# A two-layer graph network on one core: node order and loads ahead of the edge check, a re-dealt message sum in layer 0, and layer 1's pass as loops with four row buffers

## What is computed

```python
edge_index = jnp.stack([src, dst])
h = jnp.maximum(_layernorm(x, axis=-1), 0.0)
x = x + _L0_gnn_ref(h, ..., node_type_3, src, dst, edge_type_6, 4)
h = jnp.maximum(_layernorm(x, axis=-1), 0.0)
x = x + _L1_gnn_ref(h, edge_index, W, att_src, att_dst, bias, gamma, beta)
```

## Time and profile before

| what | value |
|---|---|
| median of 3 runs | 4574.36 us (4572.99 to 4576.31) |
| the profiled execution | 4572.91 us, its span 4571.2 us |
| busy share of the span | PE 57%, DVE 66%, ACT 34%, POOL 49% |
| mean granted TensorE clock | 0.789 |

### The profile page before, as it was taken

The page is one execution under the profiler, slowest core; times in us unless marked ns, Lnnn a source line. Parts: engine busy times, 40 slices in busy tenths (PEclk is TensorE's granted clock), DMA queues, the critical chain, the costliest instruction groups (busy, mean ns, idle before and its releaser), DMA issues. The chain is left out here.

```text
span 4571.2 us, 55327 instructions
## 1 busy us (share of the span) xinstructions
PE 2583.8 (57%) x10078; PEld 1666.5 (36%) x10079; DVE 3014.4 (66%) x6013; ACT 1552.4 (34%) x3956; POOL 2235.5 (49%) x2256
## 2 busy tenths in 40 slices
PE   0099956666666761000477776666355556656553
PEld 0055533433443430000255554343244444444432
DVE  3344445555555556999899997766466666666667
ACT  0234433333333332320133333333234343443443
POOL 1422257777777770000233333222477777777751
PEclk9999977777777675555699998998678777777776
DMA  6356699999999993000466664000466666666652
GB/s 205 107 229 257 260 305 312 313 312 314 312 312 314 312 312 91 0 0 0 137 198 193 200 195 130 17 16 16 94 183 193 187 192 186 192 195 187 192 156 91
DMA packets 584267, 847.44 MB, mean 185 GB/s; under 512 B 137427, under 2 KB 478815, under 8 KB 577301
## 3 DMA queue, kind: packets, MB, share of 16 engines
q0 software_dynamic: 128032, 450.69, 30.8%
q1 hardware_dynamic: 456110, 395.43, 27.7%
HBM read 549.59 MB, written 297.50 MB: 185 GB/s over the span
## 5 line engine op out<-in xcount | busy, mean ns | idle before, releaser
L1804 POOL DMA_INDIRECT g_rows<-x1t,srci x880 | 850.0, 966 | 286.7 <-issue 258.1
L903 POOL DMA_INDIRECT rows<-kv,kvi x880 | 838.6, 953 | 287.8 <-issue 246.9
L949 PE MATMUL psD<-qs,hot 128*128 x1760 | 703.6, 528 | 256.1 <-DVE prod L990 188.7
L990 DVE TENSOR_TENSOR prod<-rows,psD 128x256 f32<-128x256 f32 x880 | 365.6, 417 | 481.3 <-DMA rows<-kv,kvi 329.2
L1240 POOL TENSOR_TENSOR wv<-vrows,wgt 128x1024 f32<-128x1024 f32 x110 | 220.2, 2002 | 846.0 <-DMA vrows<-val_v 669.3
L1958 PE MATMUL g_psM<-g_rows,g_hot 128*128 128x264 f32 x1760 | 558.9, 471 | 78.7 <-DVE g_rows L2076 69.6
L949 PEld LDWEIGHTS psD<-qs,hot 128*128 128x128 f32 x1760 | 385.3, 253 | 522.5 <-issue 316.7
L1320 PE MATMUL psM<-wv,vhot 128*128 128x260 f32 x1760 | 445.3, 396 | 146.7 <-DVE run L1339 139.8
L1958 PEld LDWEIGHTS g_psM<-g_rows,g_hot 128*128 128x128 f32 x1760 | 383.8, 229 | 170.8 <-issue 96.3
L969 ACT ACTIVATE off<-psB,npiota 128x256 f32<-128x256 f32 x440 | 207.8, 472 | 688.6 <-PE psB L940 686.3
L1320 PEld LDWEIGHTS psM<-wv,vhot 128*128 128x128 f32 x1760 | 317.8, 190 | 274.1 <-DVE run L1339 227.5
(11 more groups left out here) (395 smaller groups left out, 4324.5 us busy)
## 6 DMA issues: line engine op xcount, KB each, us to landing
val_v<-rows SPq DMA_DIRECT2D x220, 512.0 KB, 5.2
vrows<-val_v SPq DMA_DIRECT2D x220, 512.0 KB
sums_v<-g_run SPq DMA_DIRECT2D x110, 528.0 KB
g_drow<-drow_v SPq DMA_DIRECT2D x55, 512.0 KB
rows<-kv,kvi POOLq DMA_INDIRECT x880, 5.1
g_rows<-x1t,srci POOLq DMA_INDIRECT x880
g_ndt<-nodeb SPq DMA_DIRECT2D x440, 6.0 KB
hsort<-blank SPq DMA_DIRECT2D x4, 1690.0 KB, 14.4
```

Source lines behind the costliest of these rows:

```text
L903: nc.gpsimd.indirect_dma_start(out=rows[:, k], out_offset=None, in_=table, in_offset=bass.IndirectOffsetOnAxis(ap=index[:, i * SLOTS + k:i ...
L949: nc.tensor.matmul(psD[:, k % 4, 0:cols], hot[:, t % 2, j * P:(j + 1) * P], node[:, ds(blk[t], 1)].rearrange("p o d -> p (o d)"), start=Tr ...
L990: ins = nc.vector.tensor_tensor(prod[:, k % 4], rows[:, k, 0:D], psD[:, k % 4, 0:D], ALU.mult)
L1804: nc.gpsimd.indirect_dma_start(out=rows[:, i % NBUF, k, 0:ROW1], out_offset=None, in_=dr["x1t"], in_offset=bass.IndirectOffsetOnAxis(ap=v[ ...
```

## The change

Four parts:

1. **Order and loads of the prologue.** The node types and `x` are now loaded by ACT's queue in `consts`; the blank fill of `hsort` by four DMAs is gone, and 5 indirect DMAs write only the rows that no node fills. The places of the nodes are worked out in `order_edges`, ahead of the sortedness test. In `prepare_edges` DVE starts with the node statistics; POOL scatters 24 blocks of nodes, then fetches the 4 record tiles, then scatters the other 25; SP loads the projection's weights there instead of at the head of `project`.
2. **Layer 0's sum.** The last of the four `vhot` groups moves from DVE to ACT (four Abs into `vfar`, one Relu). DVE's adds now stand in two runs of four, not four runs of two, and POOL's `weigh` waits until the `vhot` groups of that half turn are done on DVE.
3. **Layer 1's pass.** `walk` writes the first and the last chunks out and puts 48 chunks in a hardware loop of 12 turns with four chunks each (SP, ACT, PE and DVE loop over the steps 2 to 49, POOL over the chunks 4 to 51). There are four row buffers and four index buffers `ids`, filled by one more DMA a chunk; semaphores are split so that most waits of a chunk compare with `i`, `i + 1` or `q + 1`.
4. **Tables in one place.** Several SBUF tables share their room (`early`, `ex = sq`, `raw` in `stage`); `rank_edges` works in 20 pieces instead of 16, but does not run on these inputs.

The core of the diff:

```diff
 SB = 51
+PADS = 5
 HROW = D + 4
 HB = 6
+EARLY = 24
 EPS = 1e-5
 SLOPE = 0.2
...
+            done(nc.gpsimd.memset(c["ti"][:], T))
+            done(nc.gpsimd.memset(xs[:, NB - 1], 0.0))
...
-        @block.sync
-        def _(sp):
-            sp.wait_ge(sem, 2)
-            for f in range(4):
-                sp.dma_start(dr["hsort"].rearrange("(s f p) d -> f p s d", p=P, f=4)[f],
-                             c["blank"][:, f].unsqueeze(1).to_broadcast([P, (SB + 1) // 4, HROW])).then_inc(c["blank_in"], 16)
+        @block.scalar
+        def _(act):
+            act.wait_ge(sem, 1)
+            act.dma_start(c["ti"][0:NB - 1, :], ntype[0:(NB - 1) * P].rearrange("(b p) -> b p", p=P)).then_inc(c["t_in"], 16)
+            act.dma_start(c["ti"][NB - 1:NB, 0:NLAST], ntype[(NB - 1) * P:N].rearrange("(b p) -> b p", b=1)).then_inc(c["t_in"], 16)
+            act.wait_ge(sem, 2)
+            act.dma_start(xs[:, 0:NB - 1], x[0:(NB - 1) * P].rearrange("(b p) d -> p b d", p=P)).then_inc(c["x_in"], 16)
+            act.dma_start(xs[0:NLAST, NB - 1], x[(NB - 1) * P:N]).then_inc(c["x_in"], 16)
...
+                    tt, tsc, stt, copy = (nc.vector.tensor_tensor, nc.vector.tensor_scalar, nc.vector.scalar_tensor_tensor, nc.vector.tensor_copy)
+                    tm = o["tm"]
+                    dve.wait_ge(c["t_in"], 32)
+                    step(copy(tf[:], c["ti"][:]))
+                    for t in range(T):
+                        step(tsc(tm[:, t], tf[:], float(t), None, ALU.is_equal))
+                        step(nc.vector.tensor_tensor_scan(count[:, t], c["ones"][0:NB], tm[:, t], 0.0, ALU.mult, ALU.add))
...
+                for k in range(PADS):
+                    nc.gpsimd.indirect_dma_start(out=dr["hsort"], out_offset=bass.IndirectOffsetOnAxis(ap=o["padi"][:, k:k + 1], axis=0),
+                                                 in_=c["blank"][:, k], in_offset=None).then_inc(s_pad, 16)
+
+                def records():
...
+                    if b == EARLY:
+                        records()
...
+                load_weights(sp, weights, given)
...
                 tt, tsc = nc.vector.tensor_tensor, nc.vector.tensor_scalar
-                dve.wait_ge(s_init, 12)
-                dve.wait_ge(s_dma, 19 * 16)
+                dve.wait_ge(c["x_in"], 32)
+                for b in range(NB):
+                    nc.vector.bn_stats(stats[:, b], xs[:, b]).then_inc(s_bn, 1)
+                dve.wait_ge(s_bn, NB)
+                for b in range(NB):
+                    nc.vector.bn_aggr(mv[:, b], stats[:, b]).then_inc(s_ag, 1)
+                dve.wait_ge(s_init, 10)
...
+                    g = NG - 1
+                    for k in range(GS):
+                        ins = nc.scalar.activation(far[:, k], c["iota"][:], ACT.Abs, scale=-1.0, bias=v["dr"][:, ds(i * SLOTS + (g * GS + k), 1)])
+                    ins.then_inc(far_done, 1)
+                    act.wait_ge(far_done, i + 1)
+                    act.wait_ge(m_done, i * V8 + 2 * g + 2)
+                    nc.scalar.activation(hot[:, g * GS:(g + 1) * GS], far[:], ACT.Relu, bias=1.0, scale=-1.0).then_inc(last_hot, 1)
+
                 def turn(i, first=False):
 
                     for g in range(NG):
+                        if g == 2:
+                            places(i)
                         beside(i, g)
                         if g >= 2:
...
+                        pool.wait_ge(hot_done, i * (NG - 1) + min(g + 1, NG - 1))
...
-                            pe.wait_ge(hot_done, i * NG + t // 2 + 1)
+                            if t // 2 < NG - 1:
+                                pe.wait_ge(hot_done, i * (NG - 1) + t // 2 + 1)
+                            else:
+                                pe.wait_ge(last_hot, i + 1)
...
-                                                ALU.is_equal).then_inc(hot_done, 1)
-
-                        if g >= 2:
-                            add(i, 2 * g - 4)
-                            add(i, 2 * g - 3)
+                    for g in range(0, NG, 2):
+                        weigh(dve, nc.vector, i, g)
+                        places(i, g)
+                        if g + 1 < NG - 1:
+                            places(i, g + 1)
+                        if g:
+                            for t in range(4):
+                                add(i, t)
                         elif not first:
-                            add(i - 1, 2 * g + 4)
-                            add(i - 1, 2 * g + 5)
+                            for t in range(4, V8):
+                                add(i - 1, t)
                 turn(0, True)
...
 NCH = NC // CH
-NBUF = 3
...
+
+    def place(n):
+        return n, n % NBUF, n // NBUF
+    for n in range(first, lo):
+        step(lambda d: place(n + d))
+    with engine.Fori(0, (hi - lo) // NBUF) as t:
+        for k in range(NBUF):
+            step(lambda d: (t * NBUF + (lo + k + d), (lo + k + d) % NBUF, t + (lo + k + d) // NBUF))
+    for n in range(hi, last):
+        step(lambda d: place(n + d))
+
+
...
+                    i, m, q = at(0)
+                    pool.wait_ge(ids_in[m], 16 * (q + 1))
                     for g in range(NGRP):
-                        if i >= NBUF:
-                            pool.wait_ge(sum_done, CV * (i - NBUF) + 2 * g + 2)
+                        if from_(i, NBUF):
+                            pool.wait_ge(sum_done[2 * g + 1], i - (NBUF - 1))
+                        pool.sem_inc(opened, 1)
                         for k in range(g * GRP, (g + 1) * GRP):
                             nc.gpsimd.indirect_dma_start(
-                                out=rows[:, i % NBUF, k, 0:ROW1], out_offset=None, in_=dr["x1t"],
-                                in_offset=bass.IndirectOffsetOnAxis(ap=v["srci"][:, i * CH + k:i * CH + k + 1], axis=0)).then_inc(got[i % NBUF], 16)
+                                out=rows[:, m, k, 0:ROW1], out_offset=None, in_=dr["x1t"],
+                                in_offset=bass.IndirectOffsetOnAxis(ap=ids[:, m, k:k + 1], axis=0)).then_inc(got[m], 16)
+                walk(pool, gather, 0, 4, 52, NCH)
 
...
+                def places(i, m, q):
+                    if from_(i, NBUF):
+                        sp.wait_ge(got[m], 16 * CH * q)
+                    sp.dma_start(ids[:, m], v["srci"][:, ds(i * CH, CH)]).then_inc(ids_in[m], 16)
...
+                def add(i, m, q, t):
+                    dve.wait_ge(sum_done[t], i + 1)
+                    if t:
+                        dve.wait_ge(run_done[t - 1], i + 1)
+                    if t % 4 == 0 and from_(i, 1):
+                        dve.wait_ge(saved[t // 4], i * 16)
                     before = run[:, t - 1] if t else base[:]
...
-                places_of_nodes(0)
-                for i in range(-2, NCH):
-                    if chunk(i):
...
+        ex = sq
         psS = tmp.enter_context(nc.psum_tensor("psS", [P, 3, 512], F32))
```

More of the change, by code:

```diff
@@ new lines, in _ @@
+                    step(nc.vector.tensor_reduce(blocks[:], over[:], AX.X, ALU.add))
+                    step(copy(end[:, 0:1], blocks[:, 0:1]))
+                    step(tt(end[:, 1:2], blocks[:, 0:1], blocks[:, 1:2], ALU.add))
+                    step(stt(out=offset[:, 1:T], in0=end[0:NB], scalar=float(P), in1=offset[:, 1:T], op0=ALU.mult, op1=ALU.add))
+                    for t in range(T):
+                        step(stt(out=count[:, t], in0=count[:, t], scalar=offset[:, t:t + 1], in1=tm[:, t], op0=ALU.add, op1=ALU.mult))
@@ L861, with edge_scores @@
 NI = NC // SLOTS
[L864 removed]
+def edge_scores(nc, c, dr, v, layer, table, index, node, width, node_in, early):
     L = layer
@@ L1732, with chunk, from_, walk @@
 SPL = 3
+def chunk(i):
+    return not isinstance(i, int) or 0 <= i < NCH
+def from_(i, n):
+    return not isinstance(i, int) or i >= n
+def walk(engine, step, first, lo, hi, last):
+    def place(n):
[7 more added lines that the diff above has]
+        step(lambda d: place(n + d))
 def attend_layer1(nc, c, dr, v):
@@ L1851, in _ @@
                     if chunk(i):
                         save(i, 1)
+                for n in range(3):
+                    places(n, n, 0)
+                sp.wait_ge(init, 5)
+                nodes(0, 0, 0)
+                nodes(1, 1, 0)
+                row_flags(0, 0, 0)
+                walk(sp, step, -2, 2, 50, NCH)
                 for u in range(2):
@@ L2139 @@
+                places_of_nodes(0, 0, 0)
+                walk(dve, step, -2, 2, 50, NCH)
+                tail = (NCH - 1, (NCH - 1) % NBUF, (NCH - 1) // NBUF)
+                add(*tail, 6)
+                add(*tail, 7)
 G7 = 7
```

718 lines of the change are left out of this document (368 added, 350 removed).

## The result

| | us |
|---|---|
| before, median of 4 runs | 4575.34 (4572.99 to 4582.33) |
| after, median of 4 runs | 4459.6 (4455.82 to 4473.02) |
| ratio | 0.975, 95% interval 0.9726 to 0.9773 |
| the profiled executions | 4572.91 and 4455.82, spans 4571.2 and 4453.9 |

The change made the kernel faster by 2.5%, 116 us, where 138 were forecast: 4459.6 lies inside the stated range (4408 to 4482) and 4.6 outside the main case's own (4415 to 4455). The later runs fell on other chips, and on one of those the very same kernel is slower than before, by 1.1%. That is the main finding of this study and stands under the experiments; first comes the trace of this chip, by the prediction's own steps.

What follows compares the result with a forecast made beforehand. DVE was taken to bound layer 0's sum, POOL's gather stream layer 1's pass, a chain the prologue. Prologue -48, sum -92, layer 1 +2 gave -138: 4436 us for the median, range 4408 to 4482.

Steps and rivals of the forecast that it cites:

- main case: Whole kernel: prologue, sum and layer 1 terms hold, 4436 us for the median, own range 4415 to 4455, chance 0.62.
- E: Rival in layer 1's pass: DVE's semaphore waits, as register operations, make DVE pass POOL's pace; +235, 4671 us, chance 0.04.
- wrong outright: Sign in layer 1's pass: POOL's gathers come to wait for anything but their own stream; no size given.
- Start of `prepare_edges`: Prologue: block starts at 41.9, 2 us earlier, bounds +5 and -11.8; by the skill's rule 0.
- First scatter: Prologue, `prepare_edges`: the first scatter to `hsort` comes 25 us after the block's start, at 66.9.
- Scatters and fetches: Prologue: 49 scatters 68.8 us, four record fetches among them 5.1, slowing beside DVE 3.5; last scatter ends at 144.3.
- rival D: Prologue gives 20 us less, by an edge path late at the fetches or scatters slowed by DVE; 4456, chance 0.09.
- Start and head of `project`: Prologue: `project` starts 10 us after the last scatter, DVE's first step 10 us later instead of 18.9.
- The sum: Layer 0's sum: DVE's turn falls from 10.69 to 9.0 us as the port wait goes; -92 us.
- Layer 1's pass: Layer 1's pass: loop register operations and one index load ahead of the first gather cost +2 us.
- The bound of +23: Layer 1's pass: upper bound if a chunk's waits and increments on POOL count as six register operations.
- The fourth buffer buys nothing: Layer 1's pass: a fourth row buffer gains nothing, since only 9.7 us in all is put to a wait for sums.

Runs made afterwards that it cites:

- the last combination: The change with nine row buffers, two `vhot` groups on ACT, layer 1's pass written out, fetches behind 24 scatters: 4429.8 us, 0.967 of before.
- the combination with the pass written out: The change with nine row buffers, two `vhot` groups on ACT, old layer 1 pass; fetches behind 24 scatters 0.967, behind 19 scatters 0.9698 of before.

## Why the prediction was right or wrong

The stages gained in the order that was forecast, and the time fell into the range. The profiled pair saved 21 us less than the 138 of the forecast: 9 of these are the prologue's, 8 the sum's, the rest is small terms of either sign. That the time fell into the range is also luck of the chip. On the other kind the same kernel is 57 us slower than before, outside of every case of the forecast but E, and there the sign came that was named for being wrong outright: POOL's gathers waited for something other than their own stream, 270 us for indices.

- **Start of `prepare_edges`**, -2: it was +0.6. `o_next` is there at 39.33 instead of 38.77 whether 6.9 MB of blank rows or 6.4 MB of `x` stand ahead. The rule of the Trainium skill that was weighed there (page "DMA: Bandwidth & Descriptors", section "Why a DMA increments its semaphore by 16 and not by 1") gave 0 for this term, and by it the trace agrees in the size; that few engines are the reason, no run here shows.
- **First scatter**, 25 us into the block: 25.3.
- **Scatters and fetches**, 77.4 us: 84.0. The step that failed is "the four record fetches now stand among them at about a gather's 1.27 each". That is their price on POOL; behind them the ring of six row buffers ran dry for 9.2 us, about half of rival D's 20. The forecast counted the issues, not what the issues put into the queue.
- **Start and head of `project`**, 10 and 10: 10.4 and 10.1.
- **The sum**, -92: -84. The mechanism was right (no port wait, PE and ACT no bound, DMA share 0.72 of 0.74 forecast); the adds were undersized, 5.07 us a turn instead of 4.78. The gate proved needless where it was taken out. Of the Trainium skill's rule on the shared port (page "SBUF — State Buffer", section "SBUF: two separate sides") the trace after shows the same as before: POOL's 1.90 us lie under adds with a PSUM operand, and no `vhot` behind the first turn is lengthened.
- **Layer 1's pass**, +2: +4 on the first chip, beside gathers of 957 instead of 946 ns that go with the new prologue and tables, for which the prediction had zero. On chip 8 the term was +162, and on chip 1 some 164 to 169 if the old pass takes there what it took on chip 8. The bound of +23 was drawn from one trace in which POOL set the pace. "The fourth buffer buys nothing" held on both kinds of chip; that the index loads, counted as one load ahead of the first gather, put every chunk of gathers behind SP's stream was the missed wait. Of the prediction's rivals, E had the right stage and side, but the wrong mechanism.
- **Beyond the sum**: -8 in the node layer (within the spread, see above), and +8.5 from the last gather to the end. Of that 4 is finish's gathers, 77.8 instead of 73.9, which vary as much between other runs (74 to 78); the 4.6 of the last chunk's drain (37.1 instead of 32.5) is not settled (33.7 in the last combination, 37.5 with the old pass on chip 8).

The terms as measured: -39 - 84 + 4 - 8 + 8.5, and 1 for what lies between, is -117.5, the difference of the two spans (-117.3) but for rounding.

## What to carry to other kernels

A new load that each chunk of a stream of gathers needs is not priced by its own duration but by what stands ahead of it in its queue; issue it first in the step. Here the late load showed no cost where the stream itself set the pace, and issuing it first gave back 123 us where it didn't. A result from one chip is a result for that kind of chip: the combination with the pass written out had 0.967 on the one kind and 0.970 on the other, the looped change 0.975 and 1.011. And large transfers put among small ones with few buffers cost the small ones' buffers, not only the issue: POOL stood after six scatters with six buffers and after nine with nine.

## What was not expected of the hardware

- Two kinds of chip: the gather stages of layer 0 and of layer 1 (written out) take 1105 to 1108 and 1117 to 1125 us on two of them, 1334 to 1377 and 1284 to 1301 on three, with the sum, the projection and finish's gathers alike and a gather landing 2.5 to 2.7 us after its start on both. Why is open.
- A gather's issue on POOL in layer 1 took 946 or 947 ns in the three traces with the old prologue and tables and 957 to 960 in the others, with the same sizes and counts.
- A dependent add on DVE starts 0.61 to 0.77 us after the one before it, an operation that doesn't need it 0.40 to 0.44 (rows above). By these rows, an estimate, putting other work between would pay 0.2 to 0.3 us each.
